# Moving one tile's load and its first products ahead of two weight rows, in a Strassen-type float32 kernel

## The chip, the cores and the metric

The kernel runs on one core of one Trainium2 chip. The metric is the time of one execution on the device, in microseconds (us). The engines named below are TensorE (PE in the profile, with its weight loads as PEld), VectorE (DVE), ScalarE (ACT), GpSimd (POOL) and SyncE (SP, which here only issues transfers). An engine followed by q, as SPq, is its instruction queue.

## The reference

```
W = weights[condition]                       # one 64 x 64 matrix for each of 64 batches
y = einsum('bct,bcd->bdt', x, W)             # x is (64, 64, 1024)
logits = y @ gate_w.T + expert_bias          # 4 experts, top 1
base = y @ W_up.T                            # W_up is 1024 x 1024
delta = LoRA of the chosen expert, rank 8
out = x + base + delta
```

All of it is float32. The kernel splits each float32 operand in a high part (rounded to the format fp32r) and a low part (what is left), and multiplies high by high, high by low and low by high.

## The kernel before, in words

Two batches are stacked to 128 rows, so a tile is 128 x 1024 of x; two tiles make a block, and there are 16 blocks. The product of a block with W_up's transpose is made with seven products of half-sized operands instead of eight (Winograd's form of Strassen's method): the operands a11, a12, a22, s1, s2, s3, s4 come from y, the weights b11, b12, b21, b22 and the sums T1 to T4 from W_up.

The weights have to be made first, in the first 36 us, while the first block already starts. W_up has eight rows of pieces (row c holds b11 and b21 of column piece c, row 4 + c holds b12 and b22). For each piece TensorE turns four 128 x 128 squares into a PSUM bank (`turn`, L815), ScalarE rounds it into the high weight (`round_piece`, L579) or copies it (`copy_b12`, L584), and VectorE subtracts that from the bank for the low part (`low_piece`, L1191). VectorE also forms the sums (`form_sum`, L1212): T1 = b12 - b11, T2 = b22 - T1, T3 = T2 - b11, T4 = b21 - T2; T2 is written into b12_sb, T3 and T4 over the banks of b11 and b21. ScalarE rounds each sum (`round_sum`, L588) and VectorE or GpSimd makes its low part (`low_sum`, L271).

The y of the first two blocks is made one half at a time (`make_first_y(t, h)`, L806: 8 matmuls of 128 x 128 on the profile, tile t, half h); ScalarE moves it out of PSUM (`move_first_y`, L541), then rounds it (`round_operand`, L546), and GpSimd or VectorE makes the low part (L292). `multiply_half` (L861) multiplies one operand with half of its weight columns. GpSimd spreads the LoRA matrix (`spread_lora`, L442 to L449) and TensorE turns it (`turn_lora`, L829).

There are eight PSUM banks, and all eight are shared out by hand to pieces, y and products. The order on each engine is written out by hand, and each step waits for semaphores: `wait_piece_read(b, c)` waits until the bank of a piece is read by all its readers, `wait_y_moved(t, h)` until a y has left its bank. The banks that matter here:

```
BANK_OF: ("b22", 1): (bank_x, 0), ("b11", 1): (y_ps, 1), ("b12", 2): (y_ps, 0),
         ("b11", 0): (bank_y, 0), ("b11", 3): (y_ps, 0), ("b12", 3): (y_ps, 1)
FIRST_Y      = [(0, 1), (0, 0), (1, 0), (1, 1), ...]
FIRST_Y_BANK = [(y_ps, 0), (y_ps, 0), (bank_x, 0), (y_ps, 0), ...]
```

So y(1,0) can only be made when b22 of row 1 has been read. In `wait_piece_read`, b11 of piece c is read once T3's low part is made (`t_stage[3][c]`), b22 once its low part and T2 are, and b12 once ScalarE has copied it.

Transfers of W_up, x and the condition pairs are issued in order on SyncE's queue; those of the condition index, the router (gate_w and lora_A) and, before the change, the expert bias on ScalarE's. A condition pair is two blocks of 64 x 64, whose addresses SyncE first reads from the index (`load_first_pair`). Row 2 and row 6 of W_up go into free slots once the pieces of rows 0 have been turned. The bias is read by VectorE in `after_p1(0, 0)` (L1292). The blocks behind the first two are in steady state and are not touched.

Of the kernel before, what the change touches and what calls it, by code (L numbers as in the profile page):

```python
# [5 lines left out]
def adaln_ffn_kernel(  # L6
# [38 lines left out]
    E, R, _ = lora_a.shape  # L45
# [24 lines left out]
    with ctx:  # L70
# [198 lines left out]
        def low_sum(eng, k, c):  # L269
            eng.wait_ge(t_stage[k][c], HIGH)  # L270
            eng.tensor_tensor(turn_target(WEIGHT_OF[k], c, 1), by_k(t_place(k, c)),  # L271
                              turn_target(WEIGHT_OF[k], c, 0).bitcast(fp32), ALU.subtract).then_inc(t_stage[k][c], 1)
# [50 lines left out]
        def _(sp):  # L323
# [8 lines left out]
            def load_first_pair(q, t):  # L332
                sp.wait_ge(index_loaded, 16)
                sp.wait_ge(pair_zero, 1)
                load_pair(q, q, t)
# [5 lines left out]
            def load_w_up(row):  # L341
                c = row % OH
                if c >= 2:
                    for b in ("b11", "b21") if row < OH else ("b12", "b22"):
                        sp.wait_ge(piece_stage[b][c - 2], TURNED)
                sp.dma_start(w_raw[:, raw_slot(row), :], w_up[row * P:(row + 1) * P, :]).then_inc(w_up_loaded[row], 16)
# [4 lines left out]
            sp.dma_start(x_sb[:, 0, :], x_pairs[0]).then_inc(x_loaded[0], 16)  # L351
            load_first_pair(0, 0)
            load_w_up(5)
            load_w_up(2)
            load_w_up(6)
            load_first_pair(0, 1)
            sp.dma_start(x_sb[:, 1, :], x_pairs[1]).then_inc(x_loaded[1], 16)
            load_w_up(3)
            load_w_up(7)
            sp.dma_start(lora_b_sb[:, :, :, :], lora_b.rearrange("e (p j) r -> p e j r", p=P)).then_inc(lora_b_loaded, 16)  # L360
            load_first_pair(1, 0)
            sp.dma_start(x_sb[:, 2, :], x_pairs[2]).then_inc(x_loaded[2], 16)
            load_first_pair(1, 1)
            sp.dma_start(x_sb[:, 3, :], x_pairs[3]).then_inc(x_loaded[3], 16)

# [160 lines left out]
        def _(act):  # L526
            act.dma_start(index_sb[:, :], cond_index.rearrange("(a n) -> a n", a=1)).then_inc(index_loaded, 16)
            act.dma_start(router_sb[0:E, :], gate_w).then_inc(router_loaded, 16)
            act.dma_start(router_sb[E:GC, :], lora_a.rearrange("e r t -> (e r) t")).then_inc(router_loaded, 16)
            act.wait_ge(bias_zero, 1)  # L530
            act.dma_start(bias_sb[:, 0:E], expert_bias.rearrange("(a n) -> a n", a=1).to_broadcast([P, E]))\
                .then_inc(bias_loaded, 16)

            def load_x(q, par, t):

# [3 lines left out]
            def move_first_y(t, h, to):  # L539
                act.wait_ge(y_done, Y_AT[t, h])  # L540
                act.activation(to[:, :], first_y_bank(t, h), ACT.Copy).then_inc(y_summed, 1)  # L541

            def round_operand(op, src, q, used):
                if used:
                    act.wait_ge(product_done[op], q)
                act.activation(hl[op][:, 0, :, :], src[:, :].rearrange("q (k n) -> q k n", n=P), ACT.Copy)\  # L546
                   .then_inc(high[op], 1)
# [29 lines left out]
            def round_piece(b, c):  # L577
                act.wait_ge(piece_stage[b][c], TURNED)
                act.activation(turn_target(WEIGHT_OF[b], c, 0), by_k(bank_of((b, c))), ACT.Copy)\  # L579
                   .then_inc(piece_stage[b][c], 1)  # L580

            def copy_b12(c):
                act.wait_ge(piece_stage["b12"][c], TURNED)
                act.activation(b12_sb[:, c, :], bank_of(("b12", c)), ACT.Copy).then_inc(piece_stage["b12"][c], 1)  # L584

            def round_sum(k, c):
                act.wait_ge(t_stage[k][c], FORMED)
                act.activation(turn_target(WEIGHT_OF[k], c, 0), by_k(t_place(k, c)), ACT.Copy).then_inc(t_stage[k][c], 1)  # L588
# [47 lines left out]
            move_first_y(0, 1, a12)  # L636
            act.wait_ge(y_summed, Y_AT[0, 1])
            round_operand("a12", a12, 0, False)
            copy_b12(1)
            round_piece("b22", 1)  # L640
            move_first_y(0, 0, a11)
            round_gate_difference()
            round_sum(3, 0)
            act.wait_ge(y_summed, Y_AT[0, 0])
            round_operand("a11", a11, 0, False)
            copy_b12(2)
            round_sum(2, 1)
            round_piece("b11", 2)
            move_first_y(1, 0, a21)
            round_sum(3, 1)  # L650
            move_first_y(1, 1, a22)
            round_sum(4, 1)
            round_piece("b22", 2)
            round_lora()
# [123 lines left out]
        def _(pe):  # L778
# [32 lines left out]
            def turn(b, c):  # L811
                row, half = {"b11": (c, 0), "b21": (c, 1), "b12": (OH + c, 0), "b22": (OH + c, 1)}[b]
                pe.wait_ge(w_up_loaded[row], 16)
                for k in range(KH):
                    mm = pe.transpose(bank_of((b, c))[:, k * P:(k + 1) * P],  # L815
                                      w_raw[:, raw_slot(row), half * HALF + k * P:half * HALF + (k + 1) * P], ident[:, :])
                mm.then_inc(piece_stage[b][c], 1)
# [15 lines left out]
            def wait_piece_read(b, c):  # L833
                if b == "b11":
                    pe.wait_ge(t_stage[3][c], LOW)
                elif b == "b21":
                    pe.wait_ge(t_stage[4][c], LOW)
                elif b == "b22":
                    pe.wait_ge(piece_stage[b][c], LOW)
                    pe.wait_ge(t_stage[2][c], FORMED)  # L840
                else:
                    pe.wait_ge(piece_stage[b][c], HIGH)

            def wait_y_moved(t, h):
                pe.wait_ge(y_summed, Y_AT[t, h])
# [9 lines left out]
            def multiply_half(op, n, bank, fresh):  # L855
                pe.wait_ge(low[op], 1)
                cols = slice(QUARTER + GC, WIDE) if n else slice(0, QUARTER + GC)
                dst = bank[:, n, 0:QUARTER] if n else bank[:, 0, 0:QUARTER + GC]
                for k in range(KH):
                    for a, b in ((0, 0), (0, 1), (1, 0)):  # L860
                        mm = pe.matmul(dst, hl[op][:, a, k, :], w_of[op][:, b, k, cols],  # L861
                                       start=(fresh and k == 0 and a + b == 0),
                                       stop=(k == KH - 1 and a == 1), skip_group_check=not fresh)
                if n:
                    mm.then_inc(product_done[op], 1)
# [93 lines left out]
            turn("b22", 1)  # L959
            wait_y_moved(0, 1)  # L960
            make_first_y(0, 0)
            wait_piece_read("b12", 1)
            turn("b11", 2)
            wait_y_moved(0, 0)
            turn("b12", 2)
            turn("b22", 2)
            wait_piece_read("b22", 1)
            make_first_y(1, 0)
            wait_piece_read("b12", 2)
            make_first_y(1, 1)  # L970
            wait_piece_read("b11", 0)
            wait_pieces("b21", 0)
            pe.wait_ge(gate_stage, LOW)
            multiply_half("a12", 0, bank_y, True)
            wait_y_moved(1, 1)
            turn("b11", 3)
            wait_piece_read("b11", 1)
            turn("b12", 3)
# [209 lines left out]
        def _(dve):  # L1188
            def low_piece(b, c):
                dve.wait_ge(piece_stage[b][c], HIGH)  # L1190
                dve.tensor_tensor(turn_target(WEIGHT_OF[b], c, 1), by_k(bank_of((b, c))),  # L1191
                                  turn_target(WEIGHT_OF[b], c, 0).bitcast(fp32), ALU.subtract)\
                   .then_inc(piece_stage[b][c], 1)

            def form_sum(k, c):
                if k == 1:
                    dve.wait_ge(piece_stage["b12"][c], HIGH)
                    dve.wait_ge(piece_stage["b11"][c], HIGH)
                    a, b = b12_sb[:, c, :], bank_of(("b11", c))
                elif k == 2:  # L1200
                    dve.wait_ge(t_stage[1][c], FORMED)
                    dve.wait_ge(piece_stage["b22"][c], HIGH)
                    a, b = bank_of(("b22", c)), t_place(1, c)
                elif k == 3:
                    dve.wait_ge(t_stage[2][c], FORMED)
                    dve.wait_ge(piece_stage["b11"][c], LOW)
                    a, b = t_place(2, c), bank_of(("b11", c))
                else:
                    dve.wait_ge(t_stage[2][c], FORMED)
                    dve.wait_ge(piece_stage["b21"][c], LOW)  # L1210
                    a, b = bank_of(("b21", c)), t_place(2, c)
                dve.tensor_tensor(t_place(k, c), a, b, ALU.subtract).then_inc(t_stage[k][c], 1)  # L1212
# [140 lines left out]
            form_sum(3, 0)  # L1353
            low_piece("b11", 1)
            low_piece("b21", 1)
            form_sum(1, 1)
            low_piece("b22", 1)
            form_sum(2, 1)
            form_sum(4, 0)
            form_sum(3, 1)  # L1360
            low_sum(dve, 3, 0)
            form_sum(4, 1)
            form_sum(1, 2)
            low_sum(dve, 3, 1)
            low_piece("b11", 2)
            low_sum(dve, 4, 1)
            form_sum(2, 2)
            low_piece("b22", 2)
# [241 lines left out]
```

## Time and profile before

| | |
|---|---|
| median of 3 runs | 401.36 us (400.51 to 402.53) |
| the profiled execution | 400.69 us |
| its span, first to last instruction | 398.9 us |
| TensorE busy | 392.9 us (99% of the span) |
| VectorE busy | 314.5 us (79%) |
| ScalarE busy | 114.7 us (29%) |
| GpSimd busy | 139.9 us (35%) |

The span is that of the instructions; the time has some 2 us around it. Busy shares are averages over the span. In the first 40 us VectorE and ScalarE are much busier than the average, since the weights are made there.

### The profile page before, as it was taken

To read this page: it belongs to the slowest core of one execution; us is meant where nothing else is said; L and a number is where in the kernel's file an instruction comes from. 1 tells how busy PE (TensorE), PEld (TensorE's weight loads), DVE (VectorE), ACT (ScalarE), POOL (GpSimd) and SP (SyncE) were. 2 spreads that over 40 slices of the span, in tenths; PEclk is the share of its full clock that TensorE was granted. 3 is DMA by queue.
4 is the path that set the end of the run, shared out by engine and by line. 5 is a ranking of instruction groups with operands and counts; after the bars stand their busy time and mean duration, and the time that the engine had idled before them with its cause. 6 is when DMAs were issued, how large, how long until landed. Compare 5 with 4: busy or idle time off the path is not lost.

```text
span 398.9 us, 9766 instructions
## 1 busy us (share of the span) xinstructions
PE 392.9 (99%) x3451; PEld 359.5 (90%) x3451; DVE 314.5 (79%) x719; ACT 114.7 (29%) x226; POOL 139.9 (35%) x121
## 2 busy tenths in 40 slices
PE   7999999999999999999999999999999999999997
PEld 7899998989989899898989899898998989898996
DVE  4899678989886886869878698767868688786885
ACT  5996211433122140223213131131402223030420
POOL 1687202528123170504505072140804135050620
PEclk9999999999999999999999999999999999999999
DMA  7920230411315024231223213150142302223102
GB/s 255 362 59 2 108 118 28 144 76 60 133 42 179 29 76 145 79 138 48 75 94 110 107 56 115 46 191 26 59 158 79 120 33 97 105 93 119 55 31 102
DMA packets 20993, 39.39 MB, mean 99 GB/s; under 512 B 7494, under 2 KB 7750, under 8 KB 20970
## 3 DMA queue, kind: packets, MB, share of 16 engines
q1 hardware_dynamic: 17600, 27.40, 19.0%
q10 hardware_dynamic: 3370, 11.69, 8.6%
q8 instruction: 14, 0.23, 0.3%
q14 instruction: 9, 0.07, 0.1%
HBM read 22.30 MB, written 16.78 MB: 98 GB/s over the span
## 4 chain that ended last, share of the span: by engine, by line
PE 96%; DMA 1%; SPq 1%; ACT 1%; issue 0%; DVE 0%
PE bank_y L883 23%; PE bank_x L883 23%; PE bank_b L883 11%; PE bank_c L934 10%; PE bank_c L1087 5%; PE bank_b L1087 4%; PE y_ps L792 3%; PE bank_x L861 2%; PE bank_x L792 2%; PE bank_y L792 2%; PE bank_c L883 1%; DMA cond_pair<-in_L_cond_weights_dram 1%; PE bank_x L889 1%; PE bank_b L889 1%; PE bank_y L889 1%; PE bank_c L889 1%
## 5 line engine op out<-in xcount | busy, mean ns | idle before, releaser
L546 ACT ACTIVATE hl_a<-a 128x512 fp32r<-128x512 f32 x34 | 21.5, 633 | 105.0 <-DVE a L1414 102.5
L883 PE MATMUL bank_x<-w_a,hl_a 128*128 128x256 f32 (+1 forms) x384 | 51.2, 289 | 0.0
L883 PE MATMUL bank_y<-w_s,hl_s 128*128 128x292 f32 (+1 forms) x384 | 50.9, 288 | 0.0
L883 PEld LDWEIGHTS bank_x<-w_a,hl_a 128*128 128x128 f32 x384 | 49.3, 188 | 0.8 <-issue 0.3
L307 POOL TENSOR_TENSOR s_sum<-a 128x512 f32<-128x512 f32 x9 | 14.0, 1559 | 101.1 <-DVE a L1414 98.0
L883 PEld LDWEIGHTS bank_y<-w_s,hl_s 128*128 128x128 f32 x384 | 49.3, 188 | 0.1
L883 PE MATMUL bank_y<-w_a,hl_a 128*128 128x292 f32 x360 | 47.7, 288 | 0.0
L883 PE MATMUL bank_b<-w_s,hl_s 128*128 128x512 f32 x192 | 47.6, 397 | 0.0
L883 PEld LDWEIGHTS bank_y<-w_a,hl_a 128*128 128x128 f32 x360 | 46.6, 188 | 0.3
L307 POOL TENSOR_TENSOR s_sum<-a,a_even 128x512 f32<-128x512 f32 x7 | 11.5, 1636 | 98.4 <-DVE a_even L1414 98.4
L883 PE MATMUL bank_x<-w_s,hl_s 128*128 128x292 f32 x336 | 44.7, 289 | 0.0
L934 PE MATMUL bank_c<-w_s,hl_s 128*128 128x512 f32 x168 | 44.1, 409 | 0.0
L883 PEld LDWEIGHTS bank_x<-w_s,hl_s 128*128 128x128 f32 x336 | 43.0, 188 | 0.1
L883 PEld LDWEIGHTS bank_b<-w_s,hl_s 128*128 128x128 f32 x192 | 34.9, 188 | 6.7
L934 PEld LDWEIGHTS bank_c<-w_s,hl_s 128*128 128x128 f32 x168 | 29.4, 188 | 11.9 <-issue 5.8
L1288 DVE TENSOR_TENSOR x_sb<-bank_b,x_sb 128x512 f32<-128x512 f32 x32 | 21.8, 682 | 19.2 <-PE bank_b L883 16.4
L292 DVE TENSOR_TENSOR hl_s<-s_sum,hl_s 128x512 fp32r<-128x512 f32 x30 | 35.4, 1217 | 0.8 <-ACT hl_s L546 0.8
L546 ACT ACTIVATE hl_s<-s_sum 128x512 fp32r<-128x512 f32 x32 | 20.2, 633 | 48.1 <-POOL s_sum L307 38.2
L546 ACT ACTIVATE hl_s<-a 128x512 fp32r<-128x512 f32 x32 | 19.5, 628 | 34.1 <-POOL a L315 23.4
L1284 DVE TENSOR_TENSOR x_sb<-bank_y,x_sb 128x512 f32<-128x512 f32 x40 | 27.1, 679 | 1.2 <-PE bank_y L883 1.1
L1284 DVE TENSOR_TENSOR x_sb<-bank_x,x_sb 128x512 f32<-128x512 f32 x40 | 27.0, 676 | 0.3
L320 POOL TENSOR_TENSOR a<-a,s_sum 128x512 f32<-128x512 f32 x16 | 24.1, 1508 | 7.6 <-DVE hl_a L292 7.0
(199 smaller groups left out, 656.0 us busy)
## 6 DMA issues: line engine op xcount, KB each, us to landing
out_dram<-x_sb SPq DMA_DIRECT2D x63, 256.0 KB, 2.0
x_sb<-in_x_dram ACTq DMA_DIRECT2D x22, 512.0 KB, 3.8
x_sb<-in_x_dram SPq DMA_DIRECT2D x10, 512.0 KB, 3.3
w_raw<-in_L_ffn_W_up_dram SPq DMA_DIRECT2D x8, 512.0 KB, 5.8
cond_pair<-in_L_cond_weights_dram SPq DMA_DIRECT2D x64, 16.0 KB, 2.0
out_dram<-x_sb SPq DMA_DIRECT2D x2, 128.0 KB, 1.9
router_sb<-in_L_ffn_lora_A_dram ACTq DMA_DIRECT2D x1, 128.0 KB
lora_b_sb<-in_L_ffn_lora_B_dram SPq DMA_DIRECT2D x1, 128.0 KB, 5.2
```

The source lines that it names most:

```text
L292: eng.tensor_tensor(hl[op][:, 1, :, :], by_k(src[:, :]), hl[op][:, 0, :, :].bitcast(fp32), ALU.subtract)\
L307: eng.tensor_tensor(s1_sum[:, :], a21[:, :], second[:, :], ALU.add).then_inc(s1_added, 1)
L320: eng.tensor_tensor(a12[:, :], a12[:, :], s2_sum[:, :], ALU.subtract).then_inc(s4_added, 1)
L546: act.activation(hl[op][:, 0, :, :], src[:, :].rearrange("q (k n) -> q k n", n=P), ACT.Copy)\
L792: mm = pe.matmul(bank[j * STRIP:(j + 1) * STRIP, b, d * QUARTER:(d + 1) * QUARTER], cond_pair[rows, 2 * par + t, at:at + STRIP], strips(x_ ...
L861: mm = pe.matmul(dst, hl[op][:, a, k, :], w_of[op][:, b, k, cols], start=(fresh and k == 0 and a + b == 0), stop=(k == KH - 1 and a == 1), ...
L883: mm = pe.matmul(dst, hl[op][:, a, k, :], w[:, b, k, cols], start=(fresh and k == 0 and a + b == 0), stop=(k == KH - 1 and a == 1), skip_g ...
L889: return pe.matmul(dst, z_t[t][:, :], src, start=False, stop=True, skip_group_check=True)
L934: mm = pe.matmul(bank_c[:, 0, :], hl["s4"][:, a, k, :], w_of["s4"][:, b, k, 0:BANK], start=(k == 0 and a + b == 0), stop=(k == KH - 1 and ...
L1087: mm = pe.matmul(bank[:, 0, 0:QUARTER], left[:, a, k, :], right[:, b, k, :], start=(fresh and k == 0 and a + b == 0), stop=(k == 1 and a = ...
L1284: return dve.tensor_tensor(wide(x_part(par, t, half)), bank[:, :, 0:QUARTER], wide(x_part(par, t, half)), ALU.add)
L1288: return dve.tensor_tensor(x_part(par, t, half), bank[:, 0, :], x_part(par, t, half), ALU.add)
```

## The change

On SyncE's queue x of tile 1 and its condition pair are loaded ahead of W_up's rows 2 and 6, and the transfer of the expert bias is issued there, behind x of tile 2, and no more on ScalarE's queue at the start. On TensorE y(1,0) and y(1,1) and a12's first half product come ahead of the turns of row 2 (b11, b12, b22). On ScalarE the rounding of T3's piece 0 comes ahead of the copy of b12's piece 1, the moves of y(1,0) and y(1,1) ahead of the steps of row 2. On VectorE the low part of T3's piece 0 comes ahead of T1's piece 1, and b11's piece 2 ahead of T3's piece 1.

```diff
             sp.dma_start(x_sb[:, 0, :], x_pairs[0]).then_inc(x_loaded[0], 16)
             load_first_pair(0, 0)
             load_w_up(5)
+            sp.dma_start(x_sb[:, 1, :], x_pairs[1]).then_inc(x_loaded[1], 16)
+            load_first_pair(0, 1)
             load_w_up(2)
             load_w_up(6)
-            load_first_pair(0, 1)
-            sp.dma_start(x_sb[:, 1, :], x_pairs[1]).then_inc(x_loaded[1], 16)
             load_w_up(3)
...
             sp.dma_start(x_sb[:, 2, :], x_pairs[2]).then_inc(x_loaded[2], 16)
+            sp.wait_ge(bias_zero, 1)
+            sp.dma_start(bias_sb[:, 0:E], expert_bias.rearrange("(a n) -> a n", a=1).to_broadcast([P, E]))\
+              .then_inc(bias_loaded, 16)
             load_first_pair(1, 1)
...
-            act.wait_ge(bias_zero, 1)
-            act.dma_start(bias_sb[:, 0:E], expert_bias.rearrange("(a n) -> a n", a=1).to_broadcast([P, E]))\
-                .then_inc(bias_loaded, 16)
...
             round_operand("a12", a12, 0, False)
+            round_sum(3, 0)
             copy_b12(1)
             round_piece("b22", 1)
             move_first_y(0, 0, a11)
             round_gate_difference()
-            round_sum(3, 0)
             act.wait_ge(y_summed, Y_AT[0, 0])
             round_operand("a11", a11, 0, False)
+            round_sum(2, 1)
+            move_first_y(1, 0, a21)
+            move_first_y(1, 1, a22)
+            round_piece("b11", 2)
             copy_b12(2)
-            round_sum(2, 1)
-            round_piece("b11", 2)
-            move_first_y(1, 0, a21)
             round_sum(3, 1)
-            move_first_y(1, 1, a22)
             round_sum(4, 1)
...
             make_first_y(0, 0)
-            wait_piece_read("b12", 1)
-            turn("b11", 2)
-            wait_y_moved(0, 0)
-            turn("b12", 2)
-            turn("b22", 2)
             wait_piece_read("b22", 1)
             make_first_y(1, 0)
-            wait_piece_read("b12", 2)
+            wait_y_moved(0, 0)
             make_first_y(1, 1)
             wait_piece_read("b11", 0)
             wait_pieces("b21", 0)
             pe.wait_ge(gate_stage, LOW)
             multiply_half("a12", 0, bank_y, True)
+            wait_piece_read("b12", 1)
+            turn("b11", 2)
             wait_y_moved(1, 1)
+            turn("b12", 2)
+            turn("b22", 2)
+            wait_piece_read("b12", 2)
             turn("b11", 3)
...
             low_piece("b21", 1)
+            low_sum(dve, 3, 0)
             form_sum(1, 1)
             low_piece("b22", 1)
             form_sum(2, 1)
             form_sum(4, 0)
             form_sum(3, 1)
-            low_sum(dve, 3, 0)
             form_sum(4, 1)
+            low_piece("b11", 2)
+            low_sum(dve, 3, 1)
             form_sum(1, 2)
-            low_sum(dve, 3, 1)
-            low_piece("b11", 2)
             low_sum(dve, 4, 1)
```

## Rows read from the trace of the kernel before

**Rows 1.** The page: busy us (share of the span) and instructions of each engine.

```profile
PE 392.9 (99%) x3451; PEld 359.5 (90%) x3451; DVE 314.5 (79%) x719; ACT 114.7 (29%) x226; POOL 139.9 (35%) x121
```

**Rows 2.** Waits of weight loads, 0 to 45 us: us in total, times, longest.

```profile
PEld y_ps L815 <- ACT a L541: 0.6, 1, 0.6
...
PEld bank_y L815 <- ACT b_sb L584: 0.2, 1, 0.2
```

**Rows 3.** Timeline of weight loads: start, length, engine, line, operation, tiles, count.

```profile
8.83 0.42 PEld L815 LDWEIGHTS y_ps<-ident,w_raw 128*128 128x128 f32 x4 [1.19 <-issue]
...
10.52 0.97 PEld L806 LDWEIGHTS y_ps<-cond_pair,x_sb 128*128 128x128 f32 x8 [0.84 <-DMA x_sb<-in_x_dram]
...
15.47 0.97 PEld L806 LDWEIGHTS bank_x<-cond_pair,x_sb 128*128 128x128 f32 x8
...
17.25 1.64 PEld L861 LDWEIGHTS bank_y<-w_a,hl_a 128*128 128x128 f32 x12
18.84 0.93 PEld L815 LDWEIGHTS y_ps<-ident,w_raw 128*128 128x128 f32 x8
19.74 1.65 PEld L861 LDWEIGHTS bank_x<-w_a,hl_a 128*128 128x128 f32 x12
...
21.79 0.47 PEld L829 LDWEIGHTS bank_c<-ident,lora_b 128*128 128x128 f32 x4
...
25.56 0.52 PEld L806 LDWEIGHTS bank_b<-cond_pair,x_sb 128*128 128x128 f32 x4
```

**Rows 4.** Timeline of ScalarE.

```profile
11.72 0.60 ACT L541 ACTIVATE a<-y_ps 128x512 f32<-128x512 f32 x1 [0.59 <-PE y_ps L806]
...
12.88 0.58 ACT L584 ACTIVATE b_sb<-bank_y 128x512 f32<-128x512 f32 x1
13.36 0.59 ACT L579 ACTIVATE w_s<-bank_x 128x512 fp32r<-128x512 f32 x1
```

**Rows 5.** Timeline of VectorE.

```profile
10.03 0.69 DVE L1212 TENSOR_TENSOR bank_y<-b_sb,bank_y 128x512 f32<-128x512 f32 x1
...
13.49 0.69 DVE L1212 TENSOR_TENSOR t_sb<-b_sb,y_ps 128x512 f32<-128x512 f32 x1 [1.59 <-ACT b_sb L584]
...
14.70 0.68 DVE L1212 TENSOR_TENSOR b_sb<-bank_x,t_sb 128x512 f32<-128x512 f32 x1
...
16.49 0.68 DVE L271 TENSOR_TENSOR w_s<-bank_y,w_s 128x512 fp32r<-128x512 f32 x1
...
18.28 0.68 DVE L271 TENSOR_TENSOR w_s<-y_ps,w_s 128x512 fp32r<-128x512 f32 x1
...
20.68 0.68 DVE L1191 TENSOR_TENSOR w_s<-bank_c,w_s 128x512 fp32r<-128x512 f32 x1
```

**Rows 6.** Timeline of GpSimd.

```profile
19.94 0.40 POOL L443 COPY lora_b<-lora_b 128x256 f32<-128x256 f32 x1
...
21.10 0.40 POOL L449 COPY lora_b<-lora_b 128x256 f32<-128x256 f32 x1
```

**Rows 7.** Two stretches: busy us by engine, clock, DMA share, GB/s.

```profile
5.90:9.50 3.60, 2.48 (x24) 2.10 (x23) 3.32 (x7) 2.25 (x7) 0.00 (x0) 1.00 0.78 254
9.50:13.10 3.60, 2.97 (x26) 2.73 (x25) 2.40 (x6) 2.95 (x6) 1.33 (x2) 1.00 1.03 420
```

**Rows 8.** DMA: ScalarE's queue from 5.9 to 9.5 us; three issues, us to landing.

```profile
q10 hardware_dynamic: 142, 0.00, 2.0%
...
bias_sb<-n_L_ffn_expert_bias_dram ACTq DMA_DIRECT2D x1, 2.0 KB, 7.6
...
x_sb<-in_x_dram SPq DMA_DIRECT2D x1, 512.0 KB, 5.1
...
x_sb<-in_x_dram SPq DMA_DIRECT2D x1, 512.0 KB, 3.5
```

**Rows 9.** Timeline of SyncE's queue: the issues of x of tiles 1 and 3.

```profile
10.14 0.59 SPq L357 DMA_DIRECT2D x_sb<-in_x_dram  x1
...
20.09 0.58 SPq L364 DMA_DIRECT2D x_sb<-in_x_dram  x1
```

## The prediction

> **What bounds the kernel now.** I read the page's busy line first: TensorE (PE) is busy for 392.9 of 398.9 us, 99% [rows 1]. So the kernel is as long as TensorE's work plus its few idle microseconds. The timeline and the waits of TensorE's weight loads tell where those lie [rows 2, 3]: up to 19.7 us they are 1.2 us for W_up's row 1 (the profile puts it down to "issue"; the matmul behind it waited for the row), 0.8 us for x of the first tile and its condition pair, and 0.6 and 0.2 us for ScalarE. Behind 20 us I found no stall of TensorE behind another engine. The whole change lies in these first 20 us, so I follow TensorE's timeline there [rows 3] beside those of ScalarE, VectorE and GpSimd [rows 4 to 6]. Whatever delay TensorE has gathered when it starts a11's first half product (19.74 us) it keeps to the end, as there is no idle time behind it to swallow it.
>
> Three steps of before are needed. (a) The y of tile 1's first half, y(1,0), starts at 15.47 us; it overwrites bank_x, where W_up's piece b22 of row 1 stands, and that is free only when VectorE's form_sum(2, 1) has read it: 14.70 + 0.68 = 15.38 us [rows 3, 5]. (b) Meanwhile TensorE turned b11, b12 and b22 of row 2. (c) VectorE runs without idle time from 13.49 us on [rows 5].
>
> **Part 1: expert bias leaves the start.** It is 2 KB, but took 7.6 us to land from its issue at 2.0 us [rows 8]. From 5.9 to 9.5 us, ScalarE's queue carries 142 tiny packets that hold next to no bytes, and in this stretch the core receives 254 GB/s; in the 3.6 us after it, with that queue empty, 420 [rows 7, 8]. (420 - 254) GB/s x 3.6 us = 0.60 MB, or 1.4 us of the loads queued there: row 1, x of tile 0, its pair, row 5. Bounds for what leaves with the bias: nothing (the slow stretch has another cause) and 1.4 us. I take the upper end, since the later 256-byte packets of the condition pairs, in the 420 GB/s stretch, slow nothing, and slow stretch and tiny packets begin and end together. A rule of the Trainium skill speaks against it: DMA: Bandwidth & Descriptors, section "Why small descriptors are slow (HBM only)", gives a small packet a fixed overhead of about 3 cycles. By an estimate from that page the 8 packets of each of 16 engines cost less than one 4 KB packet, so the bias would be worth nothing and the sum would be +3.3 us in place of +1.9; the trace, 254 against 420 GB/s, does not look so.
>
> With it: row 1 has landed when the gate's turns end (7.64 us, which is 8.83 less the 1.19 us of idle time [rows 3]), so that wait of 1.2 us is gone. Two turns at 0.45 us end at 8.5; y(0,1) waited for x and its pair until 10.52; with 1.4 us less queued it starts at 9.15. The turn of b12 row 1 then needs VectorE's gate rows, done by about 10.1 us (form_sum(3, 0) starts behind them at 10.03 [rows 5]), and row 5, which was in time for 11.5 before (y(0,1)'s 10.52 plus 0.95) and comes 1.4 us earlier now: it starts at 10.2, b22 row 1 follows, then y(0,0) from 11.1 to 12.0.
>
> **Part 2: y(1,0) and y(1,1) directly behind y(0,0).** Loading is no problem. x of tile 1 took 5.1 us from its issue at 10.14 us and landed at 15.24 [rows 8, 9]. Without rows 2 and 6 ahead of it (0.5 MB each at 420 GB/s, 1.25 us each) that is 12.7, and 11.3 without the bias too; its pair, issued right behind, is there within about a microsecond. Rows 2 and 6 take its place and land by 15.2; they are needed from 17.9. But step (a) has not changed: bank_x must be read by form_sum(2, 1), and its chain gets one instruction longer. On ScalarE, round_sum(3, 0) now stands ahead of copy_b12(1): one more step of 0.5 us, the distance of two instructions in [rows 4]. The chain: move of y(0,1) 1.20 us behind its first weight load (10.52 to 11.72), so at 10.35; a12 rounded at 10.98; round_sum(3, 0) 11.5 to 12.1; on VectorE low_sum(3, 0) at 12.15, then form_sum(1, 1), low_piece(b22, 1) and form_sum(2, 1) at its 0.60 us pace, at 12.75, 13.35 and 13.95, the last done at 14.63. y(1,0) starts 0.09 us later, as before (15.38 to 15.47): 14.7. TensorE stands still from 12.0 to 14.7, 2.7 us, where before it turned row 2. VectorE has lost nothing by then, since low_sum(3, 0) left its old place at 16.49.
>
> **Part 3: the turns of row 2 behind a12's first half.** From 14.7: two y at 0.89 us (15.47 to 17.25), the product at 1.59 (17.25 to 18.84), three turns at 0.42: they end at 19.35. Their results are now asked for at once. b12 of row 2, turned at about 19.2, must be copied out of y_ps (ScalarE rounds b11 first: 18.8 to 19.3, copies to 19.9) before b11 of row 3 may be turned: 19.95, an idle 0.6 us. And b12 of row 3 needs y_ps's other bank, free after low_sum(3, 1). VectorE began that at 18.28 [rows 5]; now it is queued behind low_piece(b11, 2) and needs ScalarE's round_sum(3, 1), which comes third behind the turns, 19.8 to 20.45. So low_sum(3, 1) runs 20.45 to 21.15 and the turn starts at 21.2: 0.85 us idle. With 0.45 for the turn a11's first half product starts at 21.65, against 19.74: **+1.9 us**. By idle time: before 1.2 + 0.8 + 0.2 + 0.6 + 0.1 = 2.9; after 0.65 + 2.7 + 0.6 + 0.85 = 4.8.
>
> **What rides along.** VectorE comes out 2.2 us late (20.45 against 18.28), 0.3 more than TensorE. Its tightest due time behind is low_piece(b22, 2), done 21.36, before the LoRA turn at 21.79 [rows 3, 5]: 0.4 us of cover become 0.1. GpSimd's lora_b pieces end at 21.50 [rows 6], 0.3 us ahead of the same turn. round_lora now follows round_sum(3, 1) on ScalarE by three steps, so at 21.3; with 0.5 us for it and the three GpSimd steps (19.94 to 21.50, 1.6 us) they end at 23.4, the turn being due at 21.79 + 1.9 = 23.7. Both hold narrowly; if not, 0.1 to 0.5 us are added. The bias, moved, costs SyncE one issue of about 0.5 us behind x of tile 2; its packets may hold up the last pair and x of tile 3 by the 1.4 us of part 1. These feed y(3,0), begun at 25.56 us [rows 3], and x of tile 3 lands at 23.6 (issued 20.09, 3.5 us) [rows 8, 9], 2.0 us ahead, plus the 1.9 by which y(3,0) is late: cover enough. ScalarE's dropped wait and issue free time in which it only waited: nothing. The reordered VectorE steps low_piece(b11, 2) and low_sum are as many as before: nothing.
>
> **The sum.** The profiled execution took 400.69 us (span 398.9), plus 1.9 is 402.6. It lies 0.7 below the median of the three runs; on 401.36 the forecast is **403.3 us**.
>
> **Rivals.**
> (1) The bias is worth nothing at the start. Then y(0,1) stays at 10.52, y(1,0) starts at 16.1 and the sum is +1.9 + 1.4 = +3.3: 404.7. For it: a queue of bytes so small is an odd brake, and the slow stretch could come from the start itself. Chance 0.17.
> (2) Not slower: the bank_x chain is quicker. If ScalarE is never late, low_sum(3, 0) starts right behind low_piece(b21, 1), three steps of 0.60 behind the 10.03 of [rows 5], at 11.83; three more steps, 0.68 and 0.09 put y(1,0) at 14.4, and if row 3's two turns meet their banks free as in before, 1.45 us of waits go as well: +1.9 - 0.3 - 1.45 = +0.15, 401.5. It decides once y(1,0) begins before 14.5 and round_sum(3, 1) is done by 19.5. Against it: VectorE's order makes 14.4 a floor, and ScalarE has three instructions in a row behind the turns. Chance 0.17, a quarter of it faster by over 0.5%.
> (3) TensorE's clock falls in the 2.7 us pause. No row has such a pause; the longest, 1.19 us [rows 3], left the granted clock at its upper level, 2.4 GHz (1.00 [rows 7]). If it fell to 1.2 GHz for the work up to 19.35 (4.6 us), up to 4.6 us would be added: 408; down to none. The Trainium skill, TensorE: Matmul & The Clock Gate, section on the HAM clock gate, says the array goes back to half rate after idling; this trace does not show it. Chance 0.06.
> (4) My forecast, +1.2 to +2.8 us, 402.5 to 404.2. Chance 0.60.
>
> **Chances and range.** 0.5% is 2.0 us, about what a measurement of this kernel can tell from no change. My forecast lies on that bound: half of case 4, nearly all of 1 and 3 are slower (0.30 + 0.16 + 0.06 = 0.52); 0.04 faster; 0.44 the same. The range takes in rivals 1 and 2 with the medians' scatter of 1 us: 400.9 to 405.3, leaving out the clock case and the edges.
>
> **What would show it.** After: no wait of TensorE for row 1 at 8 us; over 350 GB/s from 6 to 9 us; y(0,1) near 9.2; a wait of some 2.7 us ahead of y(1,0), ended by VectorE's form_sum into b12_sb; waits of 0.6 and 0.85 us ahead of the turns of b11 and b12 of row 3; a11's first half near 21.65; nothing new behind. The prediction is wrong if TensorE makes y(1,0) before 14 us, if the 1.2 us wait stays, or if a wait for GpSimd or the late bias appears past 23 us.

## The result, and the profile after

The changed kernel takes 404.63 us (median of 6 runs, 403.07 to 405.31) against 401.05 us (6 runs): a ratio of 1.0078, 95% interval 1.0061 to 1.0096. It is slower by 3.6 us, and clearly so. The forecast was 403.3 us, range 400.9 to 405.3. The profiled execution took 405.31 us, the longest of the six, with a span of 403.5; the one before, 400.69, is among the shortest of its six. So the two traces lie further apart (4.6 us by the spans) than the medians (3.6).

The page of the changed kernel, busy time and the granted clock in 40 slices, answers to [rows 1]:

```profile
PE 395.5 (98%) x3451; PEld 361.8 (90%) x3451; DVE 315.0 (78%) x719; ACT 115.1 (29%) x226; POOL 139.8 (35%) x121
...
PEclk9899999999999999999999999999999999999999
```

TensorE's work is the same 3451 instructions, yet it is busy 2.6 us longer, and one slice has an 8 in its clock. The waits of its weight loads up to 60 us, against [rows 2]:

```profile
PEld bank_x L806 <- DVE w_s L1191: 2.7, 1, 2.7
...
PEld y_ps L815 <- DVE w_s L271: 0.8, 1, 0.8
PEld y_ps L806 <- DMA x_sb<-in_x_dram: 0.7, 1, 0.7
PEld y_ps L815 <- ACT b_sb L584: 0.5, 1, 0.5
PEld bank_x L861 <- issue: 0.4, 1, 0.4
```

And their timeline, against [rows 3]:

```profile
9.79 0.97 PEld L806 LDWEIGHTS y_ps<-cond_pair,x_sb 128*128 128x128 f32 x8 [0.70 <-DMA x_sb<-in_x_dram]
...
15.33 0.97 PEld L806 LDWEIGHTS bank_x<-cond_pair,x_sb 128*128 128x128 f32 x8 [2.72 <-DVE w_s L1191]
16.21 1.73 PEld L806 LDWEIGHTS y_ps<-cond_pair,x_sb 128*128 128x128 f32 x8
17.82 2.51 PEld L861 LDWEIGHTS bank_y<-w_a,hl_a 128*128 128x128 f32 x12
20.28 0.49 PEld L815 LDWEIGHTS bank_y<-ident,w_raw 128*128 128x128 f32 x4
...
22.19 0.42 PEld L815 LDWEIGHTS y_ps<-ident,w_raw 128*128 128x128 f32 x4 [0.54 <-ACT b_sb L584]
23.41 0.42 PEld L815 LDWEIGHTS y_ps<-ident,w_raw 128*128 128x128 f32 x4 [0.80 <-DVE w_s L271]
23.79 1.64 PEld L861 LDWEIGHTS bank_x<-w_a,hl_a 128*128 128x128 f32 x12
...
26.66 1.48 PEld L861 LDWEIGHTS bank_x<-w_a,hl_a 128*128 128x128 f32 x12 [0.35 <-issue]
```

Read it from the top. y(0,1) starts 0.73 us earlier than before, and the 1.2 us wait for row 1 is gone. Then comes the pause of 2.72 us ahead of y(1,0). The y behind it, 0.97 us of weight loads in every other row, takes 1.73, and a12's first half 2.51 in place of 1.64. Then the two waits behind the turns. a11's first half starts at 23.79, 4.05 us later than before; its second half starts 4.44 later (26.66 against 22.22), and the span is 4.6 longer. Behind 27 us there is nothing more to find.

The chain that ends the pause, in VectorE's timeline of the changed kernel, against [rows 5]: T3's low part, form_sum(1, 1), low_piece(b22, 1), form_sum(2, 1), then, far later, low_piece(b11, 2) and T3's low_sum(3, 1), which frees the bank that b12 of row 3 is turned into.

```profile
12.77 0.69 DVE L271 TENSOR_TENSOR w_s<-bank_y,w_s 128x512 fp32r<-128x512 f32 x1 [0.31 <-ACT w_s L588]
13.38 0.68 DVE L1212 TENSOR_TENSOR t_sb<-b_sb,y_ps 128x512 f32<-128x512 f32 x1
13.97 0.68 DVE L1191 TENSOR_TENSOR w_s<-bank_x,w_s 128x512 fp32r<-128x512 f32 x1
14.57 0.68 DVE L1212 TENSOR_TENSOR b_sb<-bank_x,t_sb 128x512 f32<-128x512 f32 x1
...
21.68 0.69 DVE L1191 TENSOR_TENSOR w_a<-bank_y,w_a 128x512 fp32r<-128x512 f32 x1 [4.63 <-ACT w_a L579]
22.66 0.69 DVE L271 TENSOR_TENSOR w_s<-y_ps,w_s 128x512 fp32r<-128x512 f32 x1 [0.29 <-ACT w_s L588]
```

form_sum(2, 1) is done at 15.25 and y(1,0) starts 0.08 later. VectorE then stands idle for 4.63 us, for TensorE had turned nothing for it. The page names L1191 as what ended the pause, a neighbour of the true one; the code says that both must be done, and L1212 is the later.

Last, the granted clock by microsecond (the column before the last two) and, in the last column, GB/s:

```profile
15.00:16.00 1.00, 0.64 (x6) 0.67 (x7) 1.00 (x3) 0.63 (x1) 1.00 (x1) 1.00 1.03 410
16.00:17.00 1.00, 1.00 (x9) 1.00 (x8) 1.00 (x2) 0.44 (x1) 1.00 (x2) 0.66 1.08 346
17.00:18.00 1.00, 1.00 (x7) 1.00 (x6) 0.06 (x1) 0.16 (x1) 0.51 (x1) 0.50 1.10 387
18.00:19.00 1.00, 1.00 (x6) 1.00 (x5) 0.00 (x0) 0.60 (x1) 0.05 (x1) 0.50 0.62 209
19.00:20.00 1.00, 1.00 (x6) 1.00 (x6) 0.00 (x0) 0.00 (x0) 1.00 (x1) 0.64 0.14 33
20.00:21.00 1.00, 1.00 (x11) 1.00 (x10) 0.00 (x0) 0.00 (x0) 0.22 (x1) 1.00 0.03 3
```

TensorE's clock fell to 1.2 GHz about a microsecond behind the pause and came back before 20 us. That was the rival of the prediction with the smallest chance. Four of the six runs have a mean clock of 0.995 or 0.996 over the span and take 404.48 to 405.31 us; the other two have 1.000 and take 403.07 and 403.68.

### The profile page after: what moved, and what is told of

It reads as the page before. It is cut to its first block, busy times and chain, and to the rows that moved or that the text cites. A ratio compares the mean times of both kernels' runs of the same rounds, so it can differ in the third digit from the quotient of the medians.

```text
span 403.5 us, 9766 instructions
## 1 busy us (share of the span) xinstructions
PE 395.5 (98%) x3451; PEld 361.8 (90%) x3451; DVE 315.0 (78%) x719; ACT 115.1 (29%) x226; POOL 139.8 (35%) x121
## 4 chain that ended last, share of the span: by engine, by line
PE 95%; DMA 1%; SPq 1%; ACT 1%; issue 1%; DVE 1%
PE bank_y L883 23%; PE bank_x L883 23%; PE bank_b L883 11%; PE bank_c L934 10%; PE bank_c L1087 5%; PE bank_b L1087 4%; PE y_ps L792 3%; PE bank_x L861 2%; PE bank_x L792 2%; PE bank_y L792 2%; PE bank_c L883 1%; DMA cond_pair<-in_L_cond_weights_dram 1%; PE bank_x L889 1%; PE bank_y L861 1%; PE bank_b L889 1%; PE bank_y L889 1%
## 5 line engine op out<-in xcount | busy, mean ns | idle before, releaser
L1288 DVE TENSOR_TENSOR x_sb<-bank_b,x_sb 128x512 f32<-128x512 f32 x32 | 21.9, 684 | 19.3 <-PE bank_b L883 16.5
```

The lines of the kernel that those rows point to most:

```text
L1288: return dve.tensor_tensor(x_part(par, t, half), bank[:, 0, :], x_part(par, t, half), ALU.add)
```

## Experiments

**1. The bias alone.** The kernel before, with the bias issued late.

```diff
             sp.dma_start(x_sb[:, 2, :], x_pairs[2]).then_inc(x_loaded[2], 16)
+            sp.wait_ge(bias_zero, 1)
+            sp.dma_start(bias_sb[:, 0:E], expert_bias.rearrange("(a n) -> a n", a=1).to_broadcast([P, E]))\
+              .then_inc(bias_loaded, 16)
...
-            act.wait_ge(bias_zero, 1)
-            act.dma_start(bias_sb[:, 0:E], expert_bias.rearrange("(a n) -> a n", a=1).to_broadcast([P, E]))\
-                .then_inc(bias_loaded, 16)
```

> The kernel before with one edit: the bias is issued on SyncE's queue behind x of tile 2. Theory (bias slows the loads of the start): 5.9 to 9.5 us moves near 400 GB/s in place of 254, y(0,1) begins near 9.8 in place of 10.52, a11's first half product near 19.0 in place of 19.74, time 0.5 to 0.9 us below the kernel before (about 400.3). Rival (the slow stretch has another cause, the gain in the changed kernel comes from the order of loads): 254 GB/s stays, y(0,1) at 10.5, time unchanged at 401.05.

Measured: 402.02 us (12 runs, 400.51 to 404.3), before 401.53, ratio 1.0013 (0.9991 to 1.0034). The first half of the theory held, the second failed. Two stretches, then TensorE's weight loads:

```profile
5.90:9.50 3.60, 2.87 (x25) 2.45 (x26) 2.95 (x6) 2.75 (x9) 0.00 (x0) 1.00 1.03 405
```

```profile
9.33 0.97 PEld L806 LDWEIGHTS y_ps<-cond_pair,x_sb 128*128 128x128 f32 x8 [0.61 <-DMA x_sb<-in_x_dram]
...
16.73 0.97 PEld L806 LDWEIGHTS bank_x<-cond_pair,x_sb 128*128 128x128 f32 x8 [2.58 <-issue]
17.62 1.77 PEld L806 LDWEIGHTS y_ps<-cond_pair,x_sb 128*128 128x128 f32 x8
```

The loads of the start run at 405 GB/s and y(0,1) is 1.19 us earlier. But y(1,0) is 1.26 us later, for its x has landed only at 16.5 us (issued at 10.3, 6.2 us). The loads ahead of it had thinned out in between (242 GB/s from 12 to 13 us), and rows 3 and 7, which W_up's faster turns now let in right behind x (row 7 issued at 11.5 us in place of 12.6), moved beside it. That these two things made x late is read from the times; experiment 8 tests the first. The pause of 2.6 us again sent the clock down in five of twelve runs (402.86 to 404.3 us); the seven at full clock have a median of 401.19. The faster start only moved the wait.

**2. The pause filled, too much.** The changed kernel with matmuls of zeros ahead of y(1,0).

```diff
+            warm_up(22, bank_c[:, 0, :])
             wait_piece_read("b22", 1)
             make_first_y(1, 0)
```

> The changed kernel with 22 matmuls of zeros into the free bank_c ahead of y(1,0): TensorE works through most of the 2.7 us pause, no result is touched. Theory (the pause itself makes the clock fall to 1.2 GHz at 16.3 us): granted clock 1.00 throughout in all runs, y(1,0) to the end of row 2's turns in 4.7 us and not 6.3, time 403.2 to 403.5 in every run (1.2 us below the changed kernel's median, like its two runs at clock 1.000). Rival (the clock falls for another reason, as the phase of the run): clock 0.996 in about two of three runs, median 404.6.

Measured: 405.49 us (5 runs), ratio 1.0091 (1.0073 to 1.0109), clock 0.999 to 1.0 in every run. The clock stayed up as the theory said, the time did not fall: each call is two matmuls at 0.113 us, so the filling took 5.0 us (12.94 to 17.86) and not 2.4. I had mis-sized it; experiment 5 mends it.

**3. The bias back at the start** of the changed kernel.

> The changed kernel with the bias back on ScalarE's queue at the start. Theory: 254 GB/s or so from 5.9 to 9.5 us, y(0,1) at 10.5, y(1,0) at 16.1, time 0.7 us above the changed kernel: 405.3. Rival (bias has no part): as the changed kernel, 404.6.

Measured: 405.18 us (6 runs), ratio 1.0092 (1.0069 to 1.0115): 0.55 us above the changed kernel, near the 0.7 expected but within the scatter. In its trace 281 GB/s from 5.9 to 9.5 us, y(0,1) at 10.74, y(1,0) at 16.27, so the pause is 2.71 us long as in the changed kernel. Here the clock stayed at full speed in three of six runs, the profiled one among them (403.9 to 404.53 us against 405.84 to 406.11). The same pause, so, brings the clock down in some executions and not in others, and the means of the two kinds of run lie 1.5 (changed kernel) and 1.7 us apart.

**4. T3's low part back at its old places** on ScalarE and VectorE, the rest as changed.

```diff
-            round_sum(3, 0)
             copy_b12(1)
...
             round_gate_difference()
+            round_sum(3, 0)
...
-            low_sum(dve, 3, 0)
             form_sum(1, 1)
...
             form_sum(3, 1)
+            low_sum(dve, 3, 0)
             form_sum(4, 1)
```

> The changed kernel with T3's piece 0 rounded and its low part made at their old places on ScalarE and VectorE. Theory (bank_x's chain through round_sum, copy_b12, form_sum sets y(1,0)): y(1,0) 0.6 us earlier behind y(0,1) (4.9 us and not 5.54), pause 2.1 us, a12's first half not held up; time 0.6 us lower at the same clock, and perhaps the clock stays up: 402.8 to 404.0. Rival (something else ends the pause): y(1,0) where it was, or a12's first half now waits for T3's low part and gives it back: 404.6.

Measured: 403.93 us (6 runs, clock 0.996 in four), ratio 1.0055 (1.0036 to 1.0074): 0.7 us below the changed kernel, which the two intervals, as they overlap, do not make certain. The trace does show the step: y(1,0) starts 4.93 us behind y(0,1) and the pause is 2.12 us:

```profile
9.49 0.97 PEld L806 LDWEIGHTS y_ps<-cond_pair,x_sb 128*128 128x128 f32 x8 [0.79 <-DMA x_sb<-in_x_dram]
...
14.42 1.47 PEld L806 LDWEIGHTS bank_x<-cond_pair,x_sb 128*128 128x128 f32 x8 [2.12 <-DVE w_s L1191]
```

So the bank_x chain sets y(1,0), and drawing T3's low part forward made it one step of 0.6 us longer. The clock fell behind this shorter pause too, here within 0.5 us of its end.

**5. The pause filled to measure:** 11 calls in place of 22.

> As the filled pause before, with 11 calls of zeros in place of 22: each call is two matmuls of 0.113 us, so 2.5 us of work, which fits in the 2.7 us pause (22 calls took 5.0 us and overran it by 2.4). Theory (the pause makes the clock fall): y(1,0) where the changed kernel has it, clock at least 0.999 in every run, 403.1 to 403.7 in every run and as median. Rival (the clock falls for another reason): clock 0.996 in about two of three runs, median 404.6.

Measured: 403.13 us (12 runs, 402.61 to 403.62), ratio 1.0036 (1.0022 to 1.0051), clock 0.999 or 1.0 in all twelve. Useless work of 2.5 us makes the changed kernel 1.5 us faster.

```profile
13.02 2.54 PEld L941 LDWEIGHTS bank_c<-zeros 128*128 128x128 f32 x22
15.50 0.97 PEld L806 LDWEIGHTS bank_x<-cond_pair,x_sb 128*128 128x128 f32 x8
16.39 0.97 PEld L806 LDWEIGHTS y_ps<-cond_pair,x_sb 128*128 128x128 f32 x8
17.28 1.64 PEld L861 LDWEIGHTS bank_y<-w_a,hl_a 128*128 128x128 f32 x12
18.87 0.49 PEld L815 LDWEIGHTS bank_y<-ident,w_raw 128*128 128x128 f32 x4
```

From y(1,0) to the first turn is 3.37 us here and 4.95 in the changed kernel: 1.58 us is the clock's part, the same as the 1.5 between the medians. The changed kernel and experiments 3 and 4, with pauses of 2.1 to 2.7 us, had a lower clock in 11 of 18 runs; the two kernels with the pause filled in none of 17. So the pause, and not some phase of the run alone, lets the clock fall here.

**6. Two turns back into the pause.** b11 and b22 of row 2, whose banks are free, ahead of y(1,0); b12 stays behind a12's first half.

```diff
             make_first_y(0, 0)
+            wait_piece_read("b12", 1)
+            turn("b11", 2)
+            turn("b22", 2)
             wait_piece_read("b22", 1)
             make_first_y(1, 0)
...
             multiply_half("a12", 0, bank_y, True)
-            wait_piece_read("b12", 1)
-            turn("b11", 2)
             wait_y_moved(1, 1)
             turn("b12", 2)
-            turn("b22", 2)
```

> The changed kernel with row 2's b11 and b22 (banks free since 13.2 us) turned ahead of y(1,0), in the pause; b12 stays behind a12's first half. Theory: the pause keeps its end (y(1,0) 5.54 us behind y(0,1)), but holds 0.9 us of work, the clock falls in fewer runs; behind it 0.45 us less work ahead of b12, so a11's first half product 0.45 us earlier at the same clock; 402.8 to 403.5 where the clock stays, median 403.3. Rival (what costs is the waits for ScalarE and VectorE behind the turns, they only grow): 404.6.

Measured: 403.47 us (10 runs, clock below 0.999 in one), ratio 1.0046 (1.0027 to 1.0065). Time and clock came out as expected, but not by the steps of the theory:

```profile
15.95 0.42 PEld L815 LDWEIGHTS bank_c<-ident,w_raw 128*128 128x128 f32 x4 [2.15 <-DMA w_raw<-in_L_ffn_W_up_dram]
16.34 0.97 PEld L806 LDWEIGHTS bank_x<-cond_pair,x_sb 128*128 128x128 f32 x8
```

b22 of row 2 waited for row 6, now loaded late, until 15.95, and y(1,0) stood behind it: it started 6.43 us behind y(0,1), not 5.54. a11's first half started 12.8 us behind y(0,1), against 12.4 in experiment 5, so no gain of 0.45 us is left in this trace; what remains against the changed kernel is the clock.

**7. The transfers' orders alone.** The engines' orders of before, with the change's order of loads and the late bias.

> The kernel before with the change's orders of transfers alone: x of tile 1 and its pair ahead of rows 2 and 6, bias late; the orders on TensorE, ScalarE and VectorE are those of before. Theory (the loss lies in the engines' orders, the loads are harmless): y(0,1) at 9.4 to 9.8, b11 of row 2 has to wait for row 2 until 13.3 and b12 for row 6 until 14.4, y(1,0) at about 15.3; time within 0.5 us of before, 400.9 to 401.4, and no pause over 1.2 us. Rival (late rows 2 and 6 stall the turns): y(1,0) after 16 us, 402.5.

Measured: 401.13 us (10 runs), before 401.54, ratio 0.999 (0.9962 to 1.0018): no difference. y(0,1) starts at 10.18, later than expected, and y(1,0) at 15.71. Ahead of the turns of row 2 stand waits of the weight loads of 0.66 and 0.82 us. Their own rows name ScalarE, but its steps had ended by 13.12 and 14.09 us, 0.5 and 0.8 us before these turns began (13.65 and 14.88); the waits of TensorE's matmuls name what came last:

```profile
PE y_ps L815 <- DMA w_raw<-in_L_ffn_W_up_dram: 0.6, 1, 0.6
PE bank_y L815 <- DMA w_raw<-in_L_ffn_W_up_dram: 0.5, 1, 0.5
```

So rows 2 and 6 do come late, as I had expected, and it costs nothing in the time. The loss lies in the orders of the engines. In two of the ten runs the clock fell (403.68 and 403.9 us).

**8. x ahead of its pair.** The fault of experiment 1 was x's late issue, behind SyncE's reading of the pair's addresses. The kernel before, bias late, and:

```diff
             load_w_up(2)
             load_w_up(6)
+            sp.dma_start(x_sb[:, 1, :], x_pairs[1]).then_inc(x_loaded[1], 16)
             load_first_pair(0, 1)
-            sp.dma_start(x_sb[:, 1, :], x_pairs[1]).then_inc(x_loaded[1], 16)
```

> The kernel before with the bias late and x of tile 1 issued ahead of its pair, still behind rows 2 and 6 (the bias-late run had x issued at 10.3 us into a queue that had run dry, 242 GB/s from 12 to 13 us, and landed only at 16.5). Theory: x issued at 7.7 us lands near 14.2, y(1,0) at 14.2 to 14.4, a11's first half at 18.6, clock 1.00: 1.1 us below before, 400.0 to 400.6. Rival (something else holds x or its pair back): y(1,0) after 15.4, no gain, 401.2 or more.

Measured: 400.49 us (12 runs, 400.08 to 401.16), before 401.54, ratio 0.997 (0.9953 to 0.9987), clock 0.999 or 1.0 in all twelve. It beats both kernels: by 1.0 us the kernel before, by some 4 the changed one.

```profile
14.27 0.47 PEld L815 LDWEIGHTS bank_c<-ident,w_raw 128*128 128x128 f32 x4
14.93 0.97 PEld L806 LDWEIGHTS bank_x<-cond_pair,x_sb 128*128 128x128 f32 x8 [0.19 <-issue]
...
19.20 1.64 PEld L861 LDWEIGHTS bank_x<-w_a,hl_a 128*128 128x128 f32 x12
```

y(1,0) starts 0.54 us earlier than before, and a11's first half 0.54 too; I had expected 1.1. y(1,0) follows y(0,1) by 5.01 us, as before (4.95), so what is missing is missing at the start: y(0,1) is only 0.60 us earlier here (9.92), 1.19 in experiment 1. The loads of this execution were slower from the first: row 4 came late (a wait ahead of its turn until 6.74, 1.1 us, 0.2 before), and from 5.9 to 9.5 us the core received 377 GB/s, in experiment 1 405.

**9. The same with the bias at the start.**

> The kernel before with x of tile 1 issued ahead of its pair and the bias left at the start: the fastest version so far with the bias's part undone. Theory (both edits are needed): y(0,1) at 10.5, y(1,0) at 15.4 as in before, 401.1 to 401.8, 1 us above the version with both. Rival (the issue order alone gives the gain): 400.5.

Measured: 401.16 us (12 runs), before 401.3, ratio 0.9999 (0.9987 to 1.0012); 231 GB/s from 5.9 to 9.5 us, y(0,1) at 10.75. Together with experiment 1 this says that both edits are needed: the bias frees the start, the issue order keeps the gain.

**10. Tiny packets on the big loads' queue.** The kernel before with the bias early, but on SyncE's queue ahead of x of tile 0.

> The kernel before with the bias issued early, but on SyncE's queue ahead of x of tile 0 and so on the same queue as the big loads, in place of ScalarE's. Theory A (each tiny packet costs the DMA engine time wherever it is queued): the stretch from 5.9 to 9.5 us stays near 254 to 280 GB/s, y(0,1) near 10.5. Theory B (it is the turn-taking of two queues, tiny packets of one between big ones of the other): near 400 GB/s, and y(0,1) near 10.0, a little later than with the bias late because its issue takes 0.4 us of SyncE's queue.

**11. One packet in place of 128.**

> The kernel before with the bias loaded to one partition, one packet in place of 128, at its old place on ScalarE's queue; 127 partitions are left without bias, so part of the expert choice is left out of the result. Theory (the 128 tiny packets slow the loads): 380 GB/s or more from 5.9 to 9.5 us, y(0,1) at 9.3 to 9.9. Rival (a third transfer on ScalarE's queue is enough): 254 to 280 GB/s, y(0,1) at 10.5.

The same stretch of 10, then of 11:

```profile
5.90:9.50 3.60, 3.60 (x31) 3.32 (x30) 2.61 (x5) 2.86 (x9) 0.00 (x0) 1.00 0.91 332
```

```profile
5.90:9.50 3.60, 3.13 (x30) 2.68 (x29) 3.16 (x6) 3.37 (x10) 0.00 (x0) 1.00 1.03 397
```

With one packet the loads run at 397 GB/s and y(0,1) starts at 9.50: it is the 128 packets that slow them, not a third transfer. On the same queue they cost about half as much (332 GB/s, y(0,1) at 9.90), so neither A nor B is all of it: in these traces, one of each, the tiny packets cost something on either queue and more on ScalarE's. Three traces with them on ScalarE's queue have 231, 254 and 281 GB/s, so 332 stands clear of them. The times, 401.53 (8 runs, ratio 1.0007, 0.9985 to 1.0029) and 402.06 (8 runs, 1.0035, 1.0007 to 1.0064), say nothing on the packets, as in both x of tile 1 comes late and the clock falls in three runs of eight.

## Why the prediction was right, and where it was not

The side and the place of the loss were forecast, its size only in part: +1.9 us, measured +3.6 between the medians. 404.63 lies above the band that I gave my own forecast (402.5 to 404.2). It is inside the range only because that took in rival 1, whose 404.7 has a cause that the runs exclude; that the time stayed inside with the clock case left out is luck. By its steps:

- **The bank_x chain (part 2): right.** y(1,0) was to start 5.55 us behind y(0,1); it started 5.54 behind. The pause was forecast at 2.7 us and is 2.72. Experiment 4 takes out its new link, and the pause shrinks to 2.12.
- **The waits behind the turns (part 3): right.** 0.6 and 0.85 us forecast, 0.54 and 0.80 measured, ended by ScalarE's copy and by low_sum(3, 1).
- **The loads are harmless: right in the time** (experiment 7), though not as early as forecast: rows 2 and 6 were to land by 15.2 us, and row 6 held up its turn until 15.95 in experiment 6. In the changed kernel the turns of row 2 came at 20.28, so this did not matter.
- **The bias (part 1): the mechanism right, the term too large.** 1.4 us for y(0,1); it came 0.73 earlier, in the other traces without the early bias 0.34 (experiment 7) to 1.19 (experiment 1), and in the medians 0.55, within the scatter (experiment 3). The stretch gained nearly what I had worked out, 396 GB/s for 254, or 1.2 us of bytes. But x of tile 0 landed 7.2 us from its issue in place of 7.9, and the second block of its pair, the last that y(0,1) waits for, 4.7 in place of 5.4: 0.7 us each. I took the term from the mean flow; why the landings gained less than the bytes stays open. Rival 1, no gain at all, is out: experiments 1 and 11.
- **The clock (rival 3): the step that failed.** The sum put it at nothing, on the ground that "No row has such a pause; the longest, 1.19 us [rows 3], left the granted clock at its upper level, 2.4 GHz". A pause of more than twice that length was judged by one of 1.2 us, and got a chance of 0.06. It happened in four of six runs and cost 1.5 to 1.6 us. The size I gave it, up to 4.6 us, was too large, for the clock fell a microsecond late and was back before 20 us. The rule named there, from the Trainium skill, TensorE: Matmul & The Clock Gate, on the HAM clock gate, that the array goes back to half rate after idling, is what the trace after shows (0.50 from 17 to 19 us).
- **VectorE's cover: half right.** GpSimd and low_piece(b22, 2) were in time. Missed was the next one, low_piece(b11, 3), ahead of a11's second half: it ended 0.27 us ahead of its due time before (21.95 against 22.22), VectorE fell 0.34 us further behind than TensorE, and a wait of 0.35 us came up that every variant of the changed order has (0.25 to 0.35). The profile calls it "issue". That VectorE ends it is not shown: the load starts 0.32 us behind the end of low_piece(b11, 3) (26.34), while y(1,0) started 0.08 behind the step that freed its bank.

At full clock a11's first half stands at 22.38 us with the pause filled, 2.6 us behind before, where I had 1.9: the 0.7 between is the bias term. That the median without the clock's part, 403.13, still lies on the forecast of 403.3 is luck, from the scatter of before: its profiled execution is at its fast end (400.69, medians 401.05 to 401.54), and a difference from there overstates the medians' difference.

## What to carry to other kernels

Moving work ahead pays only if its own inputs are ready: before it is moved past other work, look up when its output buffer is free, not only when its data has landed. Here the x came 3 us early and the bank did not, and the turns that had covered the wait were sent behind it. A pause of TensorE can cost more than its length, as the clock may fall behind it in a share of the runs; where it can't be avoided, useful work of any kind, or as here useless work, belongs in it.
When loads at the start get faster, follow the next load: its issue, on a queue that also computes addresses, may now be the late one.

## What the runs showed of the hardware that I had not expected

- The same pause of 2.7 us brought the clock to 1.2 GHz in four runs of six (changed kernel) and in three of six (experiment 3), and 2.1 us in four of six (experiment 4). In the changed kernel the fall came about 1 us behind the end of the pause. Long pauses are not the whole of it: the kernel before, whose longest wait in its trace is 1.2 us (apart from its first microsecond), had a mean clock of 0.995 or 0.996 in 4 of 17, 7 of 35 and 9 of 30 runs of the three series of experiments, 401.5 to 404.58 us long. Their medians lie about 1 us above those of the runs at full clock. No trace of one was kept, so what came before the fall there is not shown.
- The granted clock of the profile reads 1.00 from the start, but TensorE's first matmuls run at half pace. The first turns of the changed kernel, four weight loads each, took 0.87 us:

```profile
4.40 0.87 PEld L815 LDWEIGHTS bank_b<-ident,w_raw 128*128 128x128 f32 x4
5.25 0.87 PEld L815 LDWEIGHTS bank_y<-ident,w_raw 128*128 128x128 f32 x4
6.10 0.53 PEld L941 LDWEIGHTS bank_x<-zeros 128*128 128x128 f32 x4
```

  In the trace of before the first took 0.50 and the second 0.47:

```profile
4.39 0.50 PEld L815 LDWEIGHTS bank_b<-ident,w_raw 128*128 128x128 f32 x4
4.87 0.47 PEld L815 LDWEIGHTS bank_y<-ident,w_raw 128*128 128x128 f32 x4
```

  The pace doubles at a moment that differs from run to run: about 4.4 us in the trace of before, 6.1 in that of the changed kernel, 7.0 in that of experiment 7. VectorE's first step starts 0.54 us later in the changed kernel (6.34 against 5.80); this may be a part of the scatter of 1 us, which no run shows. So the record's 1.00 in the first microseconds is no evidence that a waiting TensorE has its full clock.
- 128 packets of 16 bytes, 2 KB in all, cost the other loads 1.2 us of their time. The Trainium skill, DMA: Bandwidth & Descriptors, "Why small descriptors are slow (HBM only)", knows a fixed overhead of about 3 cycles for a packet, by which, in the estimate of the prediction, they would be all but free; here the traces decide: 231 to 281 GB/s with them on ScalarE's queue, 376 to 405 without, 397 with a single one.
